# Tile 0 of a fused graph, scan and expert kernel in two half steps, and a new deal of the adjacency groups

## What is computed

```python
h = relu(adj @ layernorm(x) @ gcn_w + gcn_b)
h = layernorm(h) * ln_g + ln_b
xc, z = split(h @ w_in)                   # 256 channels each
u = silu(causal_conv4(xc) + conv_b)
dt = softplus((u @ w_xp)[:, :8] @ w_dt + b_dt);  B, C = (u @ w_xp)[:, 8:24], (u @ w_xp)[:, 24:]
state_t = exp(dt * A) * state_{t-1} + dt * u * B   # 16 states for each of 256 channels, along 8192 tokens
y = (sum over states of state_t * C) + u * D
x = x + (y * silu(z)) @ w_out
x = x + (top-1 of 8 experts on gelu(layernorm(x) @ W1))
```

## Time and profile before

| | |
|---|---|
| median of 3 executions | 1690.45 us (1690.26 to 1690.93) |
| the profiled execution | 1687.21 us |
| its span, first to last instruction | 1685.4 us |
| TensorE's mean granted clock | 0.931 of full speed |

### The profile page before, as it was taken

How to read it: one execution, slowest core, us unless ns; L and a number is a source line. 1 busy time by engine, 2 the same in 40 slices (tenths; PEclk the granted TensorE clock), 3 DMA queues, 4 the chain that set the end, 5 groups by cost and what they waited for, 6 DMA issues and landing times. The chain is left out here.

```text
span 1685.4 us, 16045 instructions
## 1 busy us (share of the span) xinstructions
PE 1423.9 (84%) x4115; PEld 669.4 (40%) x4115; DVE 1515.3 (90%) x1934; ACT 907.1 (54%) x1582; POOL 791.7 (47%) x395
## 2 busy tenths in 40 slices
PE   5998998888989989988988989889999887345578
PEld 2433343433433434444343434444443433122444
DVE  8047989999999999999999999999999999999953
ACT  3043546373737556473837465574838375665461
POOL 0013434544445455555545555555545545556541
PEclk9999999999999999999999999999999997666689
DMA  8878987888999898888898888888898886434630
GB/s 310 289 261 310 331 328 271 304 280 317 326 329 322 311 304 289 315 296 303 297 305 294 291 301 304 315 296 294 299 316 297 294 298 227 147 107 157 214 103 15
DMA packets 154494, 462.12 MB, mean 274 GB/s; under 512 B 19326, under 2 KB 42417, under 8 KB 154147
## 3 DMA queue, kind: packets, MB, share of 16 engines
q1 hardware_dynamic: 110786, 309.76, 52.5%
q10 hardware_dynamic: 38560, 139.48, 24.4%
...
...
## 5 line engine op out<-in xcount | busy, mean ns | idle before, releaser
L1227 PE MATMUL ps_adj<-ring,nodes 128*128 128x512 f32 x2048 | 948.8, 610 | 95.5 <-DMA ring<-adj 51.0
L511 POOL TENSOR_TENSOR h_c<-hidden,bc_ring 128x1024 f32<-128x1024 f32 x256 | 601.7, 2350 | 822.1 <-DVE inject L1097 638.0
L1007 DVE TENSOR_TENSOR_SCAN hidden<-decay,state,inject 128x512 f32<-128x512 f32 x512 | 627.4, 1267 | 27.0 <-ACT decay L591 3.1
L1227 PEld LDWEIGHTS ps_adj<-ring,nodes 128*128 128x128 f32 x2048 | 388.5, 194 | 601.4 <-issue 450.2
L591 ACT ACTIVATE decay<-dt_sb,negA 128x512 f32<-128x512 f32 x512 | 340.1, 713 | 28.9 <-issue 17.8
L1097 DVE TENSOR_TENSOR inject<-dtu_sb,bc_ring 128x1024 f32<-128x1024 f32 x256 | 313.9, 1226 | 5.1 <-DMA bc_ring<-bc_dram 4.0
L1050 DVE TENSOR_TENSOR y_sum<-y_sum,h_c 128x1024 f32<-128x1024 f32 x224 | 273.5, 1221 | 7.6 <-POOL h_c L511 4.7
L584 ACT COPY state<-hidden 128x2 f32<-128x2 f32 x255 | 49.0, 192 | 420.4 <-DVE hidden L1007 419.7
L482 POOL DMA_INDIRECT out<-o_sb,out_at x68 | 100.4, 1476 | 51.4 <-DVE o_sb L908 38.8
L477 POOL DMA_INDIRECT bins<-rec,dest x60 | 88.6, 1476 | 11.7 <-issue 9.7
L1149 PE MATMUL ps_e<-wd_ring,H 128*128 128x128 f32 x448 | 63.2, 299 | 13.2 <-ACT H L727 9.4
...
## 6 DMA issues: line engine op xcount, KB each, us to landing
ring<-adj SPq DMA_DIRECT2D x512, 512.0 KB, 5.9
bc_ring<-bc_dram ACTq DMA_DIRECT2D x256, 512.0 KB, 6.2
...
```

What stands on the lines that cost most here:

```text
L511: nc.gpsimd.tensor_tensor(h_c[:, s % 2], hidden[:, s % 2], over_halves(bc_ring[:, s % BC_RING, 1]), ALU.mult).then_inc(hc_ready, 1)
L1007: scan = nc.vector.tensor_tensor_scan(hidden[:, s % 2, h], decay[:, s % 2, h], inject[:, h], state[:, h, s:s + 1], ALU.mult, ALU.add)
L1227: last = nc.tensor.matmul(ps_adj[:, 0], nodes[:, m], ring[:, g % RING, m % GROUP], start=(m == 0), stop=(m == J - 1))
```

## The change

Tile 0 is taken in two steps of 256 tokens. There are now 17 steps m = 0 to 16: steps 0 and 1 are the halves of tile 0, step m is tile m-1. The stages begin at -3. Stage i makes the scans of step i+1, the front of step i+2, and the expert part of tile i-1 as before; so stage -3 sums the first half's adjacency, stage -2 makes its front, stage -1 its scans together with the second half's front, and stage 0 the scans of the second half together with tile 1's front. Every operation of front and scans takes `width(m)` columns. From stage 1 on a stage works at the same tiles as before.

For tile 0 a group is four products of 256 columns, loaded by two transfers with rows of 1 KB; 16 groups make a half. The bytes are the same. The tables MAIN and LEAD become PLAN, one entry a stage with (tile, first group, counts by slot); FRONT has new rows for stages -1 to 4. In stage -2 the B and C rows of the first half are fetched from slot 12 on, where they were fetched from slot 14. The fourth product of W1 goes to another bank in stages 1 and 2, behind the first Gelu.

```diff
-MAIN = {-2: EVEN, -1: (0, 1, 1, 0, 0, 1, 0, 0, 5, 1, 0, 1, 1, 1, 1, 0),
-        0: (0, 0, 0, 0, 0, 0, 0, 3, 2, 2, 3, 2, 2, 3, 3, 3),
-        1: (0, 0, 0, 2, 2, 2, 2, 2, 2, 2, 2, 2, 2, 2, 2, 2),
-        2: (0, 0, 2, 2, 2, 2, 2, 2, 2, 2, 2, 2, 2, 2, 2, 2),
-        3: (0, 3, 2, 2, 2, 2, 2, 2, 2, 2, 2, 2, 2, 2, 2, 3)}
-LEAD = {0: (4, 3, 3, 3, 3, 3), 1: (4, 3, 2), 2: (3, 3), 3: (4,)}
-FRONT = {0: (7, 7, 7, 7, 8, 8, 9, 10, 11, 12, 12, 13, 14, 15, 15, 15),
-         1: (2, 2, 3, 3, 4, 5, 6, 7, 8, 9, 10, 11, 12, 13, 14, 15),
-         2: (2, 2, 3, 3, 4, 5, 6, 7, 8, 9, 10, 11, 12, 13, 14, 15),
-         3: (1, 1, 2, 3, 4, 5, 6, 7, 8, 9, 10, 11, 12, 13, 14, 15)}
+PLAN = {-3: ((0, 0, (1,) * SLOTS),),
+        -2: ((0, 16, (0, 1, 1, 0, 0, 1, 0, 0, 5, 1, 0, 1, 1, 1, 1, 1)),),
+        -1: ((0, 30, (2,)), (1, 0, (0, 1, 1, 1, 1, 1, 1, 1, 2, 1, 2, 1, 2, 2, 2, 2))),
+        0: ((1, 21, (3, 3, 3, 2)), (2, 0, (0, 0, 0, 0, 0, 0, 0, 0, 0, 1, 1, 1, 1, 2, 2, 2))),
+        1: ((2, 10, (4, 4, 4, 3, 4, 3)), (3, 0, (0, 0, 0, 0, 0, 0, 0, 2, 1, 2, 2, 2, 2, 2, 2, 2))),
+        2: ((3, 17, (4, 4, 4, 3)), (4, 0, (0, 0, 0, 0, 2, 2, 2, 2, 2, 2, 2, 2, 2, 2, 2, 2))),
+        3: ((4, 24, (4, 4)), (5, 0, (0, 0, 2, 2, 2, 2, 2, 2, 2, 2, 2, 2, 2, 2, 2, 2))),
+        4: ((5, 28, (4,)), (6, 0, (0, 3, 2, 3, 2, 2, 2, 1, 2, 2, 0, 3, 2, 3, 0, 2))),
+        5: ((6, 29, (3,)), (7, 0, (0, 3, 2, 3, 2, 2, 2, 1, 2, 2, 1, 3, 2, 3, 0, 2))),
+        6: ((7, 30, (2,)), (8, 0, (1, 3, 2, 3, 2, 2, 2, 1, 2, 2, 1, 3, 2, 3, 1, 2)))}
+FRONT = {-1: (1, 1, 2, 3, 4, 4, 5, 6, 8, 9, 10, 11, 12, 13, 14, 15),
+         0: (4, 4, 5, 6, 7, 7, 8, 9, 11, 12, 12, 13, 14, 15, 15, 15),
+         1: (6, 6, 7, 9, 9, 9, 10, 11, 12, 12, 13, 13, 14, 15, 15, 15),
+         2: (5, 5, 6, 6, 7, 7, 8, 9, 10, 11, 11, 12, 13, 14, 15, 15),
+         3: (3, 3, 4, 4, 5, 5, 6, 7, 8, 9, 10, 11, 12, 13, 14, 15),
+         4: (1, 1, 2, 3, 4, 5, 6, 7, 8, 9, 10, 11, 12, 13, 14, 15)}
...
+        def width(m):
+            return T // 2 if m < 2 else T
+        def columns_of(m):
+            return slice(T // 2, T) if m == 1 else slice(0, width(m))
...
+                            half, pair = g // (GROUPS // 2), 2 * (g % (GROUPS // 2))
+                            part = ring[:, g % RING].rearrange("p a (b n) -> p (a b) n", b=2)
+                            for n in range(2):
+                                dma = sp.dma_start(part[:, GROUP * n:GROUP * (n + 1)],
+                                                   adj[0, pair + n, :, :, half * T // 2:(half + 1) * T // 2])
...
-                        nc.gpsimd.tensor_tensor(h_c[:, s % 2], hidden[:, s % 2],
+                        nc.gpsimd.tensor_tensor(h_c[:, s % 2, :, 0:w], hidden[:, s % 2, :, 0:w],
...
-                    for d, t in ((0, s + 2), (1, s + 2 - SLOTS)):
-                        if (mamba if d == 0 else front) and 0 <= t < SLOTS:
+                    for d, t in ((0, s + 2), (1, s + (4 if i == -2 else 2) - SLOTS)):
+                        if (mamba if d == 0 else front) and 0 <= t < (SLOTS if d == 0 else 2):
...
-                            scan = nc.vector.tensor_tensor_scan(hidden[:, s % 2, h], decay[:, s % 2, h],
-                                                                inject[:, h], state[:, h, s:s + 1],
+                            scan = nc.vector.tensor_tensor_scan(hidden[:, s % 2, h, 0:w], decay[:, s % 2, h, 0:w],
+                                                                inject[:, h, 0:w], state[:, h, s:s + 1],
...
-                            if k == 3:
-                                c.wait(xz_ready, 1 if front else 0, 4 if front else 0)
-                            product(h_bank(k), [(w1_sb[:, k], xn_cols)]).then_inc(h_done, 1)
+                            if k == 3 and f[7] > 7:
+                                c.wait(h_ready, -1, 1)
+                            elif k == 3:
+                                st.wait(xz_ready, 1 if front else 0, 4 if front else 0)
+                            product(h_bank(k, f[7] > 7), [(w1_sb[:, k], xn_cols)]).then_inc(h_done, 1)
```

More of the change, by code:

```diff
@@ L317, in stages @@
             live = lambda k: 0 <= k < TILES
[L318 removed]
+            step = lambda m: 0 <= m <= TILES
+            return dict(adjacency=step(i + 3), front=step(i + 2), mamba=step(i + 1), ffn=live(i - 1), scatter=live(i - 2),
                         batch=0 <= i - 4 < BATCHES, late=0 <= i - 5 < BATCHES)
         def bodies(eng, body):
[L322 removed]
+            for i in range(-3, TILES):
                 body(i, i % 2, **stages(i))
         def groups_at(i, s):
[L327 to L331 removed]
+            found = []
+            for tile, first, counts in PLAN.get(i, ((i + 2, 0, SHARE),)):
+                if tile < TILES:
                     at = first + sum(counts[:s])
                     found += [(tile, g) for g in range(at, at + (counts[s] if s < len(counts) else 0))]
[L334 removed]
             return found
@@ L1226, in body @@
-                        for m in (GROUP * g, GROUP * g + 1):
-                            last = nc.tensor.matmul(ps_adj[:, 0], nodes[:, m], ring[:, g % RING, m % GROUP],
-                                                    start=(m == 0), stop=(m == J - 1))
+                            pe.wait_ge(agg_ready, tile + 1)
+                        if (tile, g) == (0, GROUPS // 2):
+                            pe.wait_ge(agg_ready, 1)
+                        landed = tile * (GROUPS // RING) + g // RING + 1
@@ new lines, in body @@
+                        pe.wait_ge(ring_in[g % RING], 16 * (landed + min(landed, GROUPS // RING)))
+                        if tile == 0 and g < GROUPS // 2 and g % 2 == 0:
+                            pe.wait_ge(node_ready, g // 2 + 1)
+                        if tile == 0:
+                            first = 2 * GROUP * (g % (GROUPS // 2))
+                            part = ring[:, g % RING].rearrange("p a (b n) -> p (a b) n", b=2)
+                            for m in range(2 * GROUP):
+                                last = nc.tensor.matmul(ps_adj[:, 0, 0:T // 2], nodes[:, first + m], part[:, m],
+                                                        start=(first + m == 0), stop=(first + m == J - 1))
+                        else:
+                            for m in (GROUP * g, GROUP * g + 1):
+                                last = nc.tensor.matmul(ps_adj[:, 0], nodes[:, m], ring[:, g % RING, m % GROUP],
+                                                        start=(m == 0), stop=(m == J - 1))
```

276 lines of the change are left out of this document (141 added, 135 removed).

## The result

The changed kernel is slower. Its median is 1706.26 us (1704.29 to 1706.87) beside 1690.57 us for the kernel before; the ratio is 1.0077, with a 95% interval of 1.006 to 1.0095 (the quotient of the two medians is 1.0093). Forecast were 1675 us, and 1663 to 1689 as the range. The profiled execution spans 1704.3 us instead of 1685.4, so 18.9 us more.

A forecast was written before the change was run, and what follows sets the result against it. VectorE, busy for 90% of the span, was taken to bound the kernel. Tile 1's earlier first scan -14.5, stage 1 -2 and waits +1 made -15.5 us from a median of 1690.45: 1675 us, range 1663 to 1689.

The forecast's parts named there:

- First scan: Tile 0's first half: adjacency done at 51.0 us, first scan at 81 us (78 to 85).
- Price of a half state: VectorE in tile 0: 2.7 us a half-width state against 2.44, +8 us over 32 states (0 to +18).
- the sum for tile 0 (+10): VectorE's narrower operations: tile 0 costs it about 103 us where it had 93.
- The middle: Tile 0's second half to tile 1: 11 us stall, tile 1's first scan at 193 us, gain 14.5 us.
- The stages behind it: Stages 1 to 3 catch up late adjacency groups: -2 us in stage 1, +1 us for waits in stage 2.
- Stage 1, the hand-over: Tile 2's sum whole at 238, VectorE needs decay 8 at 238, gets it at 241: stall of 3 us.
- Stages 2 and 3, a missed wait: Stage 2 has 15 groups of tile 3 left, 32 us, needed at 36: +1 us for waits.
- The sum of it: Whole kernel: -14.5 - 2 + 1 = -15.5 us, median 1675 us.
- The last of the prediction's signs of being wrong: Stages 1 to 3 over 95 us, with VectorE waiting for ScalarE's decay.
- (b): Stages 1 and 2: late groups and TensorE's other work cost 6 us more each, 1687 us; chance 13%.
- (c): Stages 1 to 3: dearer groups, nothing overlapped; at 2.3 us a group 35 us lost, 1710 us; chance 8%.
- the 2.16 of the earlier trace: Kernel before, 113.07 to 151.9 us: 2.16 us a group while TensorE waits for the ring, DMA share 0.95.

The follow-up runs named there:

- rebalanced: Changed kernel: 15 tile 2 groups and bins' fill in stage 0, 19 tile 3 groups in stage 1, Ln before Gelu, no groups between copy and gcn; ratio 0.9953.
- groups earlier: Rebalanced kernel with tile 4's and tile 5's groups at three a slot directly behind the front's first products of stages 2 and 3; ratio 0.9971.
- both: Rebalanced kernel with groups earlier in stages 2 and 3 and 4 KB rows for tile 0's adjacency; ratio 0.9974.
- whole tile with the mended deal: Kernel before, tile 0 whole, with the rebalanced kernel's deal of groups, fill and queue order from stage 0 on; ratio 0.9978.
- the seventh experiment: Changed kernel with the front's Ln, Exp and scaling in slot 8 instead of 9 of stage 1, ahead of the experts' Gelu; ratio 1.01.
- light tile 2: Changed kernel where 13 of tile 2's 22 groups in stage 1 load and multiply only 64 of 512 columns; ratio 1.0018.

## Why the prediction was wrong, point by point

- **First scan.** Forecast 81, measured 78.5 (78.5 to 81.3 in all kernels with half steps). First half whole: 51.0 and 49.6. TensorE's five groups before w_xp, the order of the steps and the fetch went as described; right.
- **Price of a half state.** Forecast 2.7 us, measured 2.74 (scans at 120.07 and 122.81, the pair 1.38):
```profile
120.07 1.39 DVE L1038 TENSOR_TENSOR_SCAN hidden<-decay,state,inject 128x256 f32<-128x256 f32 x2
121.42 0.69 DVE L1084 TENSOR_TENSOR y_sum<-y_sum,h_c 128x512 f32<-128x512 f32 x1
122.02 0.69 DVE L1133 TENSOR_TENSOR inject<-dtu_sb,bc_ring 128x512 f32<-128x512 f32 x1
122.81 1.39 DVE L1038 TENSOR_TENSOR_SCAN hidden<-decay,state,inject 128x256 f32<-128x256 f32 x2
```
  So 16 states cost 4.8 us more than half of a whole tile's; the sum for tile 0 (+10) was right.

  The Trainium skill's fixed time of an operation (VectorE: DVE Perf Modes, the TRN2 errata) points the same way: by its 58 cycles the cut costs an estimated 4 us, by the rows 0.30 us a state, 9.6 in all. The same section says that its 58 cycles under-predict a single operation, and that an fp32 `tensor_tensor` takes (N+151)/0.96 ns; with these 151 cycles the estimate is 10 us, and this case agrees with it.
- **The middle.** Second half's scans from 135.0 instead of 130: a wait of 5.09 us for a decay behind the second copy at 88.0 (I had it at 84.7), and 2.7 us for the fetch of B and C. Tile 1 whole at 159.7 instead of 154, the stall 10.35 us (11 forecast). From that copy to tile 1's first scan 42.2 instead of 39 us; in this stretch TensorE's granted clock was 0.80, and eight w_in products took 6.24 us where they took 3.95 at the full clock. Tile 1's first scan came at 201.9 instead of 193; the range I gave for it ended at 199, and the four other profiles of the same code have 197.6 to 199.2. Mechanism right, size short by 9 us of 14.5, some 3 of which are this one profile.
- **The stages behind it: here the prediction failed.** I put -1 us on them; they cost +24. Three steps of it:
  - Stage 1, the hand-over: I had tile 2 whole 45 us after the stage's first scan, VectorE in need of its decay at 45, and the decay 3 us behind the copy: a stall of 3. Measured are 49.8, 41.7 and 4.3, so 12.4. The length of the 22 groups was not the error: with w_out they took 45.2 us, as forecast, 1.97 us a group without w_out's 1.95 (the 2.06 of the expectations counts it in). The error was their start: I let it coincide with VectorE's first scan, and TensorE was 4.55 us late. With VectorE's earlier need (3.3 us) and the longer step from copy to decay (1.3) that makes the 9 us that the stall exceeded my 3.
  - Stages 2 and 3, a missed wait: I compared numbers of groups and bytes by stage and put +1 us on waits. Measured are waits of 4.14, 2.62 and 8.33 us, where the kernel before has 1.32 and less. I followed each table by itself and never laid PLAN beside FRONT; slots 4 and 5 of one against f[0] = 5 of the other give four groups between copy and gcn, to be read from the diff alone. Nor had I asked who waits behind ScalarE's wait.
  - The front's Exp: waits of 4.55 us in stage 1 and 2.62 in stage 2, which the forecast doesn't have. The 2.62 is not the price of the FRONT row of stage 2: ten of the fourteen kernels with this row have it, each behind a wait of 0.96 to 9.06 us for the decay, and the four where the sum came in time (rebalanced, groups earlier, both, whole tile with the mended deal) wait there 0.3 us or less. So it belongs to the late hand-over. What the 4.55 us consist of stays open: the seventh experiment moved them, and light tile 2 kept them with its decay in time.
- **The sum of it.** The rest of the sum was built on "what the first scan gains comes off the end, as long as no later stage stretches". The stretching was no separate risk: with this deal tile 2's sum is whole at 251 with or without the half steps, and VectorE can't pass it. The last of the prediction's signs of being wrong, stages 1 to 3 over 95 us with VectorE waiting for ScalarE's decay, is what came.
- **The rivals.** (b), arrears paid back on the path, had the right place and half the size (12 us); (c) had the size (its 1710 for the 1706 measured) but needed a dearer group, 2.3 us, which was not there: at the 1.97 us measured in stage 1 its own sum gives 2 us. That its 1710 lies near 1706 is luck. Its sum also has a slip: it passes 15.5 us at 2.13 us a group and not at 2.15, so the 2.16 of the earlier trace rows lay well inside. Both together had 21%.
